# Cross attention: the value weighting moved from three places in a half to two, the last block's own buffer, and the output weights in a context buffer

## Chip, cores and metric

One core of one Trainium2 chip runs the whole program. The metric is device microseconds (us) of one execution; lower is better. The kernel before takes 4177.87 us (median of 3 runs, 4175.75 to 4178.8).

## What is computed

Four transformer layers on x (16 x 64 x 256, f32), each of cross attention, self attention and a feed-forward part. The change touches the cross attention alone, which all four layers run on the same 1601 context rows:

```python
q = split_heads(layernorm(x) @ Wq + bq)      # 16 heads of 16, 64 rows per batch
k = split_heads(ctx @ Wk + bk)               # 1601 keys
v = split_heads(ctx @ Wv + bv)
out = softmax(q k^T * scale [+ mask]) @ v    # 16 batches
x = x + merge_heads(out) @ Wo + bo
```

Layer 0 adds a float mask to the scores, layer 2 replaces masked scores, layers 1 and 3 have none.

## The kernel before

`cross_attention` works through 32 **halves** u (16 batches, two groups of 8 heads), each in seven **steps** i = 0 to 6. Every engine (PE, DVE, ACT, POOL) runs through the same list of steps in an order that is written out by hand; semaphores tie them together. The numbers of a half are kept in `prob` (128 x 4 x 1601). Before the weighting with the values, `prob` has to be transposed block by block: 1601 keys make 13 blocks of 128 rows, two to a step, the last step with a single block of 65 rows.

In step i of half u PE does, in this order:

1. `scores` (L474) of the next half, chunk i, in steps 0 to 3;
2. `turn` (L486): the transposes of two blocks of half u into PSUM banks 4 and 5. Its `bank(...)` waits until the copy of the blocks turned one step earlier is out of these banks;
3. `make_keys` (L502) of half u+2 in even steps, `make_values` (L516) of the next batch in odd ones. Both write bank 7 (UNIT), and each waits until what was there before has been taken out: for keys by `keys_low` (L671) on DVE, in layer 2 by the product with `kept` (L660), for values by `values_copy` (L609). In step 6 of odd halves a small `make_values` (the 65 rows) comes first, into bank 5;
4. `weighted` (L531): what is turned is multiplied with the values. Steps 0 to 6 are weighted in three bursts: blocks of steps 0 and 1 at the end of step 2, of steps 2 and 3 at the end of step 4, of steps 4, 5 and 6 at the end of step 0 of the next half, followed there by `spread_denominators` (L541).

The turned blocks are copied from PSUM to `prob_t` by `turned_copy` (L599): ACT takes steps 0 to 3, DVE steps 4 to 6. `prob_t` is a ring of four places, one for each step. DVE's order in step 4 is: the copy of the turned blocks (L599), then `keys_high` (L663), then `keys_low` (L671); in step 5: the copy (L599), the copy of the values (L609); in step 6 the copy of the 65 rows, in odd halves the small values, and keys again. In step 0 it takes the maxima of the scores (L641, L644), the low part of keys, and then `outputs` of the half before (L683, L686, L688), after which step 1's maxima follow. ACT computes the exponentials (L737) of the next half in steps 4 to 6. POOL splits the context into two parts (L810, L812) at steps 1, 3 and 5 of odd halves, in layer 2 the keys as well (L826, L828). In layer 2 DVE makes the next mask at the end of odd halves (L365, L368).

SP issues the loads. The output weights `wout` (256 KB) are loaded before the context of batch 1; `raw_ctx[0]` and `raw_ctx[1]` take turns for the context chunks. `project_out` (L563) reads `wout` from half 30, step 1 on.

The last half has bank 0 as a second place for the transposes (odd steps), its copies alternate between ACT and DVE.

Of the kernel before, what the change touches and what calls it, by code (L numbers as in the profile page):

```python
# [15 lines left out]
P = 128  # L16
B, S, D, H = 16, 64, 256, 16
HD = D // H
C = D // P
# [4 lines left out]
KT = -(-KEYS // P)  # L24
# [79 lines left out]
def by_rows(ap):  # L104
    return ap.rearrange("(c p) n -> p c n", p=P)
# [192 lines left out]
STEPS = (KT + 1) // 2  # L298
CH = len(KCH)
TURNED, HEADS, UNIT = 4, 6, 7  # L300
LAST = HALVES - 1
WEIGHTED_AT = {2: (0, 1), 4: (2, 3)}

def cross_attention(k, L, scale, mask=None, wo='Wo', bo='bo'):

# [2 lines left out]
    nc, ps, dram, cst = k.nc, k.ps, k.dram, k.cst  # L308
    name = f"L{L}_xattn_"
    st = Stage(k)  # L310
    wk, wv = (st.tile(n, [P, 2, C, D], F32R) for n in ('wk', 'wv'))
    raw_ctx = [st.tile(f"raw_ctx{i}", [P, C, KCH[0][1]]) for i in range(2)]
    ctx = st.tile("ctx", [P, 2, C, KEYS2], F32R)
    keys = [st.tile(f"keys{g}", [P, 2, KEYS2], F32R) for g in range(2)]
    wout = st.tile("wout", [P, C, D])
    mk = [st.tile(f"mk{i}", [P, KEYS]) for i in range(2)] if mask else None
    kept = st.tile("kept", [P, KEYS]) if mask == 'fill' else None
    vals = [st.tile(f"vals{i}", [P, KT, D]) for i in range(2)]
    prob = [st.tile(f"prob{i}", [P, ROWS, KEYS]) for i in range(2)]
    prob_t = st.tile("prob_t", [P, 4, 2, 512])  # L320
    q_heads = st.tile("q_heads", [P, C, P])
    q_parts = [st.tile(f"q_parts{i}", [P, 2, C, P], F32R) for i in range(2)]
    mx = st.tile("mx", [P, ROWS, CH])
# [14 lines left out]
    def width(i):  # L338
        return min(KCH[i][1], KEYS - KCH[i][0])

    def columns(i):
        return slice(KCH[i][0], KCH[i][0] + width(i))

    def ctx_chunk(b, i):
        return dram['ctx_t'][b].rearrange("(c p) n -> p c n", p=P)[:, :, columns(i)]

    def load_mask(b):
        sem = st[f'mask{b % 2}']
        if mask == 'add':
            nc.sync.dma_start(mk[b % 2][0:S, :], dram['mask_f'][b]).then_inc(sem, 16)  # L350
            nc.sync.dma_start(mk[b % 2][S:P, :], dram['mask_f'][b]).then_inc(sem, 16)
        else:
            nc.sync.dma_start(mk[b % 2][:].bitcast(I32), dram['mask_i'][b].partition_broadcast(P)).then_inc(sem, 16)
# [28 lines left out]
    def turn_bank(u, i):  # L382

        return 0 if u == LAST and i % 2 else TURNED

    def blocks(i):
        return [x for x in (2 * i, 2 * i + 1) if x < KT]

    def rows_of(x):
        return min(P, KEYS - x * P)  # L390

    def steps():


        for u in range(-2, HALVES):
            for i in range(STEPS):
                chunk = i // 2 if i % 2 == 0 and u + 2 < HALVES else None
                pairs = []
                if u // 2 + 1 < B:
                    pairs = [i // 2 + 3 * (u % 2)] if i % 2 else [6] if i == 6 and u % 2 else []  # L400
                yield u, i, u >= 0, 0 <= u + 1 < HALVES and i < CH, chunk, pairs
# [4 lines left out]
    def values_out(b, n):  # L406

        if values_by_act(n):
            return st.at('v_act', 4 * b + (0, 1, 3, 4).index(n) + 1)
        return st.at('v_dve', 3 * b + (2, 5, 6).index(n) + 1)  # L410

    def turned_out(u, i):

        if u == LAST:
            return st.at('pt_dve' if i % 2 else 'pt_act', (3 if i % 2 else 4) * u + i // 2 + 1)
        return st.at('pt_act', 4 * u + i + 1) if i < 4 else st.at('pt_dve', 3 * u + i - 3)
# [8 lines left out]
    def out_tiles(u, i):  # L425

        return [t for t in ([i - 1] if u == LAST - 1 else [i + 5]) if 0 <= t < T - 1 and (u < LAST or i == 1)]

    def ring(u, i):
        return (u * STEPS + i) % 4  # L430

    def sp():
        sp = nc.sync
        for n, tile, i in (('Wk', raw_wk, 0), ('Wv', raw_wv, 1), ('Wq', wq, 2)):
            sp.dma_start(tile, by_rows(dram[name + n])).then_inc(st[n], 16)
            sp.dma_start(first_ctx[:, :, columns(i)], ctx_chunk(0, i)).then_inc(st[f'first{i}'], 16)
        sp.dma_start(first_ctx[:, :, columns(3)], ctx_chunk(0, 3)).then_inc(st['first3'], 16)
        if mask:
            load_mask(0)
        sp.dma_start(wout[:], by_rows(dram[name + wo])).then_inc(st['wout'], 16)  # L440
        sp.dma_start(k.row[:], dram['bias_rows'][BIAS_ROWS.index(name + bo)].partition_broadcast(P)).then_inc(st['row'], 16)
        for b in range(1, B):
            if mask:
                if b >= 2:
                    sp.wait_ge(*st.at('nmx', 2 * (b - 1)))
                load_mask(b)
            for i in range(CH):
                if b > 1 or i >= 2:
                    sp.wait_ge(*st.at('ctx_lo', CH * b + i - 1))
                sp.dma_start(raw_ctx[i % 2][:, :, 0:width(i)], ctx_chunk(b, i)).then_inc(st[f'ctx{i % 2}'], 16)  # L450
        if L == 0:
            clear_sorted(k, st, zeros)

    def pe():
# [7 lines left out]
        def scores(h, i):  # L462
            b, g = h // 2, h % 2
            k0, kw = KCH[i]
            pe.wait_ge(*st.at('k_lo', CH * h + i + 1))
            if i == 0:
                pe.wait_ge(*st.at('q_lo', b + 1))
            for m, (qp, kp) in enumerate(PASSES):
                for r in range(ROWS):
                    if m == 0:  # L470
                        bank(r)
                        free[r] = st.at('s_out', ROWS * (CH * h + i) + r + 1)
                    rows = slice(32 * r, 32 * r + 32)
                    mm = pe.matmul(ps[:, r, 0:kw], q_parts[b % 2][rows, qp, g, :], keys[g][rows, kp, k0:k0 + kw],  # L474
                                   start=(m == 0), stop=(m == 2))
            mm.then_inc(st['s_mm'], 1)
# [43 lines left out]
        def weighted(u, i):  # L520
            b, g = u // 2, u % 2
            if i == 0:
                pe.wait_ge(*values_out(b, 4))
                pe.wait_ge(*values_out(b, 6))
                if u:
                    pe.wait_ge(*st.at('both', u))
            pe.wait_ge(*turned_out(u, i))
            for a, x in enumerate(blocks(i)):
                w = rows_of(x)
                for r in range(ROWS):  # L530
                    mm = pe.matmul(ps[32 * r:32 * r + 32, HEADS, g * P:(g + 1) * P],  # L531
                                   vals[b % 2][0:w, x, (ROWS * g + r) * 32:(ROWS * g + r + 1) * 32],
                                   prob_t[0:w, ring(u, i), a, r * P:(r + 1) * P], start=(x == 0), stop=(x == KT - 1))
            mm.then_inc(st['pv_mm'], 1)

        def spread_denominators(u):
# [31 lines left out]
        for u, i, attend, score, chunk, pairs in steps():  # L568
            if score:
                scores(u + 1, i)  # L570
            if attend:
                turn(u, i)
            if 6 in pairs:
                make_values(u // 2 + 1, 6)
            if chunk is not None:
                make_keys(u + 2, chunk)
            elif pairs:
                make_values(u // 2 + 1, pairs[0])
            if u == -2 and i in (2, 4):
                project_queries(i // 2 - 1)  # L580
            if u >= LAST - 1:
                for t in out_tiles(u, i):
                    project_out(t)
            if attend:
                for x in WEIGHTED_AT.get(i, ()):
                    weighted(u, x)
            if u >= 1 and i == 0:
                for x in (4, 5, 6):
                    weighted(u - 1, x)
                spread_denominators(u - 1)  # L590
        for x in (4, 5, 6):
            weighted(LAST, x)
        spread_denominators(LAST)
        project_out(T - 1)
# [1 line left out]
    def turned_copy(copy, sem, u, i):  # L596

        w, nb = rows_of(blocks(i)[-1]), len(blocks(i))
        copy(prob_t[0:w, ring(u, i), 0:nb, :], ps[0:w, turn_bank(u, i):turn_bank(u, i) + nb, :]).then_inc(st[sem], 1)  # L599

    def turned_ready(engine, u, i):
        n = u * STEPS + i
        engine.wait_ge(*st.at('t_mm', n + 1))
        if n >= 4:
            engine.wait_ge(*st.at('pv_mm', n - 3))

    def values_copy(copy, sem, b, n):
        w, nb = rows_of(blocks(n)[-1]), len(blocks(n))
# [181 lines left out]
    def pool():  # L790
# [48 lines left out]
        for u, i, attend, score, chunk, pairs in steps():  # L839
# [18 lines left out]
            if mask == 'add' and u >= 0 and u % 2 == 0 and i == 5 and b < B:  # L858
                mask_row(b)

    sp()
    pe()
    dve()
    act()
    pool()
    n = HALVES
# [875 lines left out]
def clear_sorted(k, st, zeros):  # L1742

    sp = k.nc.sync
    sp.wait_ge(*st.at('zeros', 1))
    for L in (2, 3):
        sp.dma_start(k.dram[f'sorted{L}'].rearrange("(s p) d -> p s d", p=P),
                     zeros[:].unsqueeze(1).broadcast_to([P, BLOCKS * 2, D])).then_inc(st[f'cleared{L}'], 16)
# [624 lines left out]
```

## Time and profile before

| What | Value |
|---|---|
| median of 3 runs | 4177.87 us (4175.75 to 4178.8) |
| the profiled execution | 4171.85 us |
| its span, first to last instruction | 4170.5 us |
| mean granted TensorE clock | 0.951 |
| PE busy | 3803.9 us (91%) |
| PEld (weight loads) busy | 3192.5 us (77%) |
| DVE busy | 2811.9 us (67%) |
| ACT busy | 2135.9 us (51%) |
| POOL busy | 1597.8 us (38%) |
| `weighted` L531, PE | 13312 records, 444.5 us |
| `turn` L486, PE | 6656 records, 916.3 us |
| copy of turned blocks L599, DVE | 384 records, 402.3 us |

PE is the matmul row and PEld the weight load row of the same engine; each f32 matmul in the program shows as two records. "Idle before" is the time an engine stood still ahead of an instruction, with what ended it; "issue" there means that it waited for no other engine.

### The profile page before, as it was taken

The numbers are of one execution on the slowest core, as the hardware profiler recorded it, in microseconds if no ns is written. First come the engines' busy times: TensorE is split into PE (matmuls) and PEld (weight loads), VectorE is DVE, ScalarE is ACT, GpSimd is POOL, SyncE is SP. The second block draws the span as 40 slices with busy tenths as digits, with TensorE's granted clock in tenths as the row PEclk, the third lists the DMA queues.
The fourth block names the chain that finished last, engine by engine and source line by source line (L and its number), as shares of the span: only waits on it lengthen the run. The fifth ranks groups of instructions, "written<-read, shape, count | busy, mean of one in ns | idle before, by whom it ended". The sixth has DMA issues, their size and how long they took to land. (4 is left out here: it accounts for less than half of the span.)

```text
span 4170.5 us, 102428 instructions
## 1 busy us (share of the span) xinstructions
PE 3803.9 (91%) x42956; PEld 3192.5 (77%) x42956; DVE 2811.9 (67%) x7243; ACT 2135.9 (51%) x2963; POOL 1597.8 (38%) x1647
## 2 busy tenths in 40 slices
PE   7999999854999999988999999986997999999866
PEld 6888888633888888857788888865996888888656
DVE  5777777676777777753777777755446777777544
ACT  4555555442555556533445454533654555555434
POOL 3444343201332332130666655513773333322146
PEclk9999999986999999998999999986998999999968
DMA  3122123001111111010211111102542111110035
GB/s 95 49 65 57 49 65 109 17 23 35 41 41 33 38 44 33 10 39 31 69 53 53 49 64 52 30 12 91 186 148 75 38 33 41 41 33 25 13 104 176
DMA packets 125594, 235.94 MB, mean 57 GB/s; under 512 B 9920, under 2 KB 114768, under 8 KB 121296
## 3 DMA queue, kind: packets, MB, share of 16 engines
q1 hardware_dynamic: 117744, 172.34, 13.9%
q0 software_dynamic: 7392, 57.06, 3.8%
q8 instruction: 341, 5.59, 0.5%
q14 instruction: 117, 0.96, 0.1%
HBM read 208.39 MB, written 20.97 MB: 55 GB/s over the span
## 5 line engine op out<-in xcount | busy, mean ns | idle before, releaser
L599 ACT COPY prob_t<-ps 128x1024 f32<-128x1024 f32 x512 | 518.4, 1013 | 1162.3 <-PE ps L486 1162.3
L486 PE MATMUL ps<-c_ident,prob 128*128 128x128 f32 (+1 forms) x6656 | 916.3, 279 | 12.7 <-ACT prob L737 9.9
L486 PEld LDWEIGHTS ps<-c_ident,prob 128*128 128x128 f32 (+1 forms) x6656 | 717.4, 141 | 188.9 <-issue 157.5
L737 ACT ACTIVATE prob<-prob,nmx 128x1601 f32<-128x1601 f32 x512 | 828.7, 1625 | 1.1 <-DVE nmx L650 1.1
L502 PE MATMUL ps<-ctx,wk 128*128 128x400 f32 (+1 forms) x3072 | 691.7, 361 | 21.9 <-DVE vals L609 14.1
L516 PE MATMUL ps<-wv,ctx 128*128 128x256 f32 x4992 | 704.4, 289 | 3.3 <-DVE vals L609 3.1
L516 PEld LDWEIGHTS ps<-wv,ctx 128*128 128x128 f32 x4992 | 619.9, 186 | 10.5 <-DVE vals L609 4.0
L641 DVE CUSTOM_DVE_ANT_0 prob<-ps,mk 128x400 f32<-128x400 f32 (+2 forms) x1024 | 526.2, 569 | 112.9 <-PE ps L474 110.4
L644 DVE TENSOR_SCALAR_CACHE_REDUCE prob<-ps 128x400 f32<-128x400 f32 (+2 forms) x1024 | 526.1, 569 | 90.9 <-PE ps L474 90.7
L502 PEld LDWEIGHTS ps<-ctx,wk 128*128 128x128 f32 x3072 | 534.8, 191 | 45.3 <-DVE vals L609 28.5
L599 DVE COPY prob_t<-ps 128x1024 f32<-128x1024 f32 (+1 forms) x384 | 402.3, 1048 | 239.1 <-PE ps L486 238.8
L810 POOL CAST ctx<-raw_ctx 128x804 fp32r<-128x804 f32 x240 | 205.2, 855 | 735.8 <-PE ps L502 735.8
L474 PE MATMUL ps<-keys,q_parts 32*128 32x400 f32 (+1 forms) x6144 | 474.3, 379 | 5.3
L531 PE MATMUL ps<-prob_t,vals 128*32 128x128 f32 x13312 | 444.5, 275 | 1.2 <-DVE prob_t L599 1.2
L531 PEld LDWEIGHTS ps<-prob_t,vals 128*32 128x32 f32 x13312 | 339.8, 110 | 102.2 <-issue 99.4
L812 POOL TENSOR_TENSOR ctx<-raw_ctx,ctx 128x804 fp32r<-128x804 f32 x240 | 402.8, 1678 | 19.3
L852 POOL TENSOR_TENSOR diag<-c_ident,rden 128x128 f32<-128x128 f32 x512 | 188.8, 400 | 502.5 <-DVE rden L678 502.5
L474 PEld LDWEIGHTS ps<-keys,q_parts 32*128 32x128 f32 x6144 | 274.4, 183 | 137.7 <-issue 70.3
L671 DVE SCALAR_TENSOR_TENSOR keys<-ps,cols,keys 128x400 fp32r<-128x400 f32 (+2 forms) x384 | 243.4, 634 | 129.0 <-ACT keys L743 121.8
L2108 POOL TENSOR_TENSOR parts<-raw,parts 128x1368 fp32r<-128x1368 f32 (+2 forms) x70 | 205.1, 2938 | 68.3 <-ACT parts L2033 67.7
L609 ACT COPY vals<-ps 128x512 f32<-128x512 f32 x256 | 149.5, 584 | 128.7 <-PE ps L516 128.7
L1982 PE MATMUL ps<-x_parts,parts 128*114 128x256 f32 (+1 forms) x1440 | 189.0, 289 | 14.3 <-POOL parts L2108 7.3
(350 smaller groups left out, 4313.0 us busy)
## 6 DMA issues: line engine op xcount, KB each, us to landing
raw_ctx<-in_ctx_t SPq DMA_DIRECT2D x120, 400.0 KB, 3.3
raw_ctx<-in_ctx_t SPq DMA_DIRECT2D x60, 402.0 KB, 5.1
raw_ctx<-in_ctx_t SPq DMA_DIRECT2D x60, 399.0 KB, 3.3
mk<-in_mask_f SPq DMA_DIRECT2D x32, 400.2 KB, 5.5
mk<-in_mask_i SPq DMA_DIRECT2D x16, 800.5 KB, 4.4
sorted<-zeros SPq DMA_DIRECT2D x2, 3840.0 KB, 20.6
rows<-sorted SPq DMA_DIRECT2D x30, 256.0 KB, 5.2
done<-done SPq DMA_DIRECT2D x30, 256.0 KB, 2.5
```

What stands on the lines that cost most here:

```text
L474: mm = pe.matmul(ps[:, r, 0:kw], q_parts[b % 2][rows, qp, g, :], keys[g][rows, kp, k0:k0 + kw], start=(m == 0), stop=(m == 2))
L486: mm = pe.transpose(ps[0:w, turn_bank(u, i) + a, r * P:(r + 1) * P], prob[u % 2][:, r, x * P:x * P + w], cst['ident'][:])
L502: mm = pe.matmul(ps[:, to, 0:kw], wk[:, wp, c, g * P:(g + 1) * P], ctx[:, xp, c, k0:k0 + kw], start=(c == 0 and m == 0), stop=(c == C - 1 ...
L516: mm = pe.matmul(ps[0:w, to, a * D:(a + 1) * D], ctx[:, xp, c, x * P:x * P + w], wv[:, wp, c, :], start=(c == 0 and m == 0), stop=(c == C ...
L531: mm = pe.matmul(ps[32 * r:32 * r + 32, HEADS, g * P:(g + 1) * P], vals[b % 2][0:w, x, (ROWS * g + r) * 32:(ROWS * g + r + 1) * 32], prob_ ...
L599: copy(prob_t[0:w, ring(u, i), 0:nb, :], ps[0:w, turn_bank(u, i):turn_bank(u, i) + nb, :]).then_inc(st[sem], 1)
L641: v.tensor_tensor_reduce(o, ps[:, r, 0:vw], mk[b % 2][:, k0:k0 + vw], 1.0, NEG, ALU.add, ALU.max, mx[:, r, i:i + 1]).then_inc(st['s_out'], 1)
L644: v.tensor_scalar(o, ps[:, r, 0:vw], 0.0, NEG, ALU.add, ALU.max, accum_out=mx[:, r, i:i + 1]).then_inc(st['s_out'], 1)
L671: v.scalar_tensor_tensor(keys[g][:, 1, k0:k0 + vw], ps[:, key_bank(h, i), 0:vw], k.col(name + 'bk')[:, g:g + 1], keys[g][:, 0, k0:k0 + vw] ...
L737: a.activation(prob[h % 2][:, r, :], prob[h % 2][:, r, :], ACT.Exp, bias=nmx[:, r:r + 1], accum_out=den[h % 2][:, r:r + 1]).then_inc(st['e ...
L810: p.tensor_copy(ctx[:, 0, :, columns(i)], raw).then_inc(st['ctx_own'], 1)
L812: p.tensor_tensor(ctx[:, 1, :, columns(i)], raw, ctx[:, 0, :, columns(i)].bitcast(F32), ALU.subtract).then_inc(st['ctx_lo'], 1)
```

## The change

`weighted` runs in two bursts in place of three: blocks of steps 0, 1 and 2 at the end of step 2, blocks of steps 3 to 6 at the end of step 0 of the next half. The ring of four places holds steps 0 to 5, and step 6's single block gets a tile of its own, `last_t`. The conditions on which a copy may write are counted anew. `wout` loses its tile and is loaded into `raw_ctx[0]`, behind all context chunks. The code:

```diff
-WEIGHTED_AT = {2: (0, 1), 4: (2, 3)}
+WEIGHTED_AT = {2: (0, 1, 2)}
+CARRIED = (3, 4, 5, 6)
+RING = 4
...
-    wout = st.tile("wout", [P, C, D])
+    wout = raw_ctx[0][:, :, 0:D]
...
-    prob_t = st.tile("prob_t", [P, 4, 2, 512])
+    prob_t, last_t = st.tile("prob_t", [P, RING, 2, 512]), st.tile("last_t", [P, 1, 512])
...
-    def ring(u, i):
-        return (u * STEPS + i) % 4
+    def turned(u, i):
+
+        return last_t if i == STEPS - 1 else prob_t[:, (u * (STEPS - 1) + i) % RING]
...
-        sp.dma_start(wout[:], by_rows(dram[name + wo])).then_inc(st['wout'], 16)
...
+        sp.wait_ge(*st.at('ctx_lo', CH * B - 1))
+        sp.dma_start(wout, by_rows(dram[name + wo])).then_inc(st['wout'], 16)
...
             if u >= 1 and i == 0:
-                for x in (4, 5, 6):
+                for x in CARRIED:
                     weighted(u - 1, x)
                 spread_denominators(u - 1)
-        for x in (4, 5, 6):
+        for x in CARRIED:
             weighted(LAST, x)
...
     def turned_ready(engine, u, i):
-        n = u * STEPS + i
-        engine.wait_ge(*st.at('t_mm', n + 1))
-        if n >= 4:
-            engine.wait_ge(*st.at('pv_mm', n - 3))
+        n = u * (STEPS - 1) + i
+        engine.wait_ge(*st.at('t_mm', u * STEPS + i + 1))
+        if i == STEPS - 1:
+            if u:
+                engine.wait_ge(*st.at('pv_mm', u * STEPS))
+        elif n >= RING:
+            old_u, old_i = divmod(n - RING, STEPS - 1)
+            engine.wait_ge(*st.at('pv_mm', old_u * STEPS + old_i + 1))
```

On PE, before, from step 3 of half 1 of layer 0 to the end of its step 6 (prob_14 is what is turned, vals_11 the batch's values; each matmul counts once here):

```order
L474 MATMUL ps<-keys_6,q_parts_18 128x400 x12
L486 MATMUL ps<-c_ident,prob_14 128x128 x8
L516 MATMUL ps<-wv,ctx 128x256 x12
L486 MATMUL ps<-c_ident,prob_14 128x128 x8
L502 MATMUL ps<-ctx,wk 128x400 x6
L531 MATMUL ps<-prob_t,vals_11 32x128 x16
L486 MATMUL ps<-c_ident,prob_14 128x128 x8
L516 MATMUL ps<-wv,ctx 128x256 x12
L486 MATMUL ps<-c_ident,prob_14 65x128 x4
L516 MATMUL ps<-wv,ctx 65x256 x6
L502 MATMUL ps<-ctx,wk 128x400 x6
```

The same place in the changed kernel (lines are four higher, prob_14 is now prob_13):

```order
L478 MATMUL ps<-keys_6,q_parts_18 128x400 x12
L490 MATMUL ps<-c_ident,prob_13 128x128 x8
L520 MATMUL ps<-wv,ctx 128x256 x12
L490 MATMUL ps<-c_ident,prob_13 128x128 x8
L506 MATMUL ps<-ctx,wk 128x400 x6
L490 MATMUL ps<-c_ident,prob_13 128x128 x8
L520 MATMUL ps<-wv,ctx 128x256 x12
L490 MATMUL ps<-c_ident,prob_13 65x128 x4
L520 MATMUL ps<-wv,ctx 65x256 x6
L506 MATMUL ps<-ctx,wk 128x400 x6
```

The burst of 16 between the keys of step 4 and the transposes of step 5 is gone.

On PE, in the changed kernel, the end of step 0 of the next half and what follows (before, the burst read `L531 MATMUL ps<-prob_t,vals_11 32x128 x20`):

```order
L506 MATMUL ps<-ctx,wk 128x402 x6
L535 MATMUL ps<-prob_t,vals_10 32x128 x24
L535 MATMUL ps<-last_t,vals_10 32x128 x4
L545 MATMUL ps<-diag,c_pairblk 32x128 x4
L478 MATMUL ps<-keys_7,q_parts_18 128x400 x12
```

This burst has grown by 8 matmuls; the burst at the end of step 2 has grown by 8 too, from 16 to 24.

## Rows read from the trace of the kernel before

**Rows 1.** The page's first part: busy us (share of the span) xrecords.

```profile
PE 3803.9 (91%) x42956; PEld 3192.5 (77%) x42956; DVE 2811.9 (67%) x7243; ACT 2135.9 (51%) x2963; POOL 1597.8 (38%) x1647
```

**Rows 2.** Line L531 (PEld): what ended its idle time, us, times.

```profile
  issue: 99.4, 384
```

**Rows 3.** Timeline, layer 0, odd half, steps 4 to 6 (start, us, engine, line).

```profile
322.02 0.90 PEld L486 LDWEIGHTS ps<-c_ident,prob 128*128 128x128 f32 x8
...
322.96 1.02 PEld L502 LDWEIGHTS ps<-ctx,wk 128*128 128x128 f32 x6
...
323.20 1.23 DVE L599 COPY prob_t<-ps 128x1024 f32<-128x1024 f32 x1 [0.94 <-PE ps L486]
324.25 0.81 PEld L531 LDWEIGHTS ps<-prob_t,vals 128*32 128x32 f32 x32 [0.26 <-issue]
...
324.36 0.63 DVE L663 TENSOR_SCALAR keys<-ps,cols 128x400 fp32r<-128x400 f32 x1
...
325.02 0.63 DVE L671 SCALAR_TENSOR_TENSOR keys<-ps,cols,keys 128x400 fp32r<-128x400 f32 x1
325.26 0.86 PEld L486 LDWEIGHTS ps<-c_ident,prob 128*128 128x128 f32 x8 [0.20 <-issue]
...
326.08 1.49 PEld L516 LDWEIGHTS ps<-wv,ctx 128*128 128x128 f32 x12
...
326.39 1.22 DVE L599 COPY prob_t<-ps 128x1024 f32<-128x1024 f32 x1 [0.73 <-PE ps L486]
...
327.67 0.41 PEld L486 LDWEIGHTS ps<-c_ident,prob 128*65 128x65 f32 x4
...
328.74 1.04 PEld L502 LDWEIGHTS ps<-ctx,wk 128*128 128x128 f32 x6
```

**Rows 4.** Timeline, layer 0, even half: steps 5 and 6, into the next half.

```profile
303.37 1.47 PEld L516 LDWEIGHTS ps<-wv,ctx 128*128 128x128 f32 x12
...
305.83 1.03 PEld L502 LDWEIGHTS ps<-ctx,wk 128*128 128x128 f32 x6 [0.46 <-DVE vals L609]
...
306.48 0.19 ACT L737 ACTIVATION_READ_ACCUMULATOR prob<-prob,nmx 128x1 f32 x1
...
307.88 0.86 PEld L486 LDWEIGHTS ps<-c_ident,prob 128*128 128x128 f32 x8 [0.26 <-issue]
```

**Rows 5.** Timeline, layer 0, steps 0 and 1 of an odd half.

```profile
311.14 1.90 POOL L812 TENSOR_TENSOR ctx<-raw_ctx,ctx 128x804 fp32r<-128x804 f32 x1
...
312.31 0.82 DVE L688 SCALAR_TENSOR_TENSOR XNT<-both,cols 128x64 f32<-128x64 f32 x1
...
314.63 0.21 PEld L474 LDWEIGHTS ps<-keys,q_parts 32*128 32x128 f32 x3
...
315.16 0.47 PEld L474 LDWEIGHTS ps<-keys,q_parts 32*128 32x128 f32 x9 [0.31 <-DVE mx L641]
...
315.89 0.85 PEld L486 LDWEIGHTS ps<-c_ident,prob 128*128 128x128 f32 x8 [0.26 <-issue]
```

**Rows 6.** The same of an even half: `outputs`, scores of step 2, next transposes.

```profile
718.57 0.28 DVE L688 SCALAR_TENSOR_TENSOR XNT<-both,cols 128x64 f32<-128x64 f32 x1
...
720.90 0.49 PEld L474 LDWEIGHTS ps<-keys,q_parts 32*128 32x128 f32 x12
...
721.65 0.85 PEld L486 LDWEIGHTS ps<-c_ident,prob 128*128 128x128 f32 x8 [0.26 <-issue]
```

**Rows 7.** Timeline, layer 0, half 30 (no keys or values left), steps 5 and 6.

```profile
751.71 0.86 PEld L486 LDWEIGHTS ps<-c_ident,prob 128*128 128x128 f32 x8 [0.20 <-issue]
...
754.12 0.41 PEld L486 LDWEIGHTS ps<-c_ident,prob 128*65 128x65 f32 x4 [0.85 <-DVE prob_t L599]
```

**Rows 8.** Timeline, layer 2: end of an odd half, and scores of an even half's step 2.

```profile
2107.33 1.60 POOL L812 TENSOR_TENSOR ctx<-raw_ctx,ctx 128x800 fp32r<-128x800 f32 x1
...
2109.18 0.98 DVE L365 TENSOR_SCALAR mk<-mk 128x1601 f32<-128x1601 int32 x1
...
2092.22 2.21 PE L474 MATMUL ps<-keys,q_parts 32*128 32x400 f32 x12
```

More of the change, by code:

```diff
@@ L532, in weighted @@
                                    vals[b % 2][0:w, x, (ROWS * g + r) * 32:(ROWS * g + r + 1) * 32],
-                                   prob_t[0:w, ring(u, i), a, r * P:(r + 1) * P], start=(x == 0), stop=(x == KT - 1))
+                                   turned(u, i)[0:w, a, r * P:(r + 1) * P], start=(x == 0), stop=(x == KT - 1))
             mm.then_inc(st['pv_mm'], 1)
@@ L598, in turned_copy @@
         w, nb = rows_of(blocks(i)[-1]), len(blocks(i))
-        copy(prob_t[0:w, ring(u, i), 0:nb, :], ps[0:w, turn_bank(u, i):turn_bank(u, i) + nb, :]).then_inc(st[sem], 1)
+        copy(turned(u, i)[0:w, 0:nb, :], ps[0:w, turn_bank(u, i):turn_bank(u, i) + nb, :]).then_inc(st[sem], 1)
     def turned_ready(engine, u, i):
-        n = u * STEPS + i
-        engine.wait_ge(*st.at('t_mm', n + 1))
-        if n >= 4:
-            engine.wait_ge(*st.at('pv_mm', n - 3))
+        n = u * (STEPS - 1) + i
[6 more added lines that the diff above has]
+            engine.wait_ge(*st.at('pv_mm', old_u * STEPS + old_i + 1))
     def values_copy(copy, sem, b, n):
```

## The prediction, written before the changed kernel was run

> **What bounds the kernel now.** I read the page's first part first. PE is busy for 91% of the span, no other engine for more than 67% [rows 1]. So the first question is what PE's order costs. The busy share itself cannot say what a moved burst is worth; for that I read the timeline of one half, engine by engine, and ask at each instruction what let it start. The halves are regular: the times of one, told from the start T of the transposes of step 4 (322.02 in [rows 3]), recur in the others within a few hundredths.
>
> In [rows 3] the reader is to see two things. First, the weighting burst stands between two gaps in which PE waits for nobody: 0.26 us before it and 0.20 after it. The source view counts such gaps before a burst: 99.4 us in 384, three for each of 128 halves [rows 2]. Second, while the burst runs, DVE works off a chain of three: the copy of the turned blocks (ends T+2.41), `keys_high`, and `keys_low`, which ends at 325.65 = T+3.63. The transposes of step 5 need the first of these, the values of step 5 the third, since they write the bank that the keys were in. Both start later than that today (T+3.24 and T+4.06), so neither waits. The burst is their cover.
>
> **What is removed.** In each half the burst of step 4 goes, with one pair of gaps: 0.26 + 0.20 = 0.46 us. Its 0.81 us of loads do not go. Half of them, 0.41, are added at the end of step 2, the other half at the end of step 0, where a burst with its gaps stands anyway. If PE had nothing to wait for, keys to transposes would cost a gap of up to 0.1, and a half would gain about 0.37.
>
> **What takes its place, layers 0, 1 and 3.** I follow PE from T. The keys of step 4 are loaded by T+1.96. The transposes of step 5 would come now, but banks 4 and 5 are free only when DVE's copy is done, T+2.41. From the end of such a copy to PE's next start takes 0.06 (326.39 + 1.22 = 327.61, then 327.67 [rows 3]), so they start at T+2.47. That copies cannot be beaten is seen in half 30, where nothing stands between: the next transposes start 2.41 after the ones before, and DVE's copy is named as what they waited for [rows 7]. Next, PE reaches the values 0.82 later, as today (325.26 to 326.08), at T+3.29, and waits for `keys_low`: T+3.63 + 0.06 = T+3.69. Today they start at T+4.06, of which 0.82 is moved work, so T+3.24 would be even. **The loss at this point is 0.45 us**: all of the gaps' 0.46 is given back, and as much again.
>
> In even halves nothing mends it: the keys of step 6 start 2.46 after the values of step 5 and are already released by DVE's copy of the values [rows 4], so the whole 0.45 goes through. In odd halves the transposes of step 6 wait today for the copy (327.67). Changed, that copy starts T+3.60 and is out by T+4.82, while PE gets there at about T+5.2; before it was T+5.65, less 0.82. So 0.39 is left of the 0.45. The small values and the keys behind them run on PE's own time. The exponentials do not enter: they end 306.67, and the transposes that need them start 307.88, 1.21 later [rows 4]; 0.4 of that is used up. Each layer has 15 even and 15 odd halves with keys and values to make (0 to 29): 15 x 0.45 + 15 x 0.39 = 12.6 us, three layers 37.8.
>
> **What is swallowed.** The 0.41 added in step 0 lies ahead of `outputs` on DVE, and of the scores of step 2 on PE. In odd halves PE stalls there today: from the scores' first load to the next transposes takes 1.26 us [rows 5], in even halves 0.75 [rows 6]. The cause is L688: 0.82 us in the odd half, 0.28 in the even; it ends at 313.13, just after POOL's L812 at 313.04. L812 follows the keys of step 0, not the burst. So the burst may grow by 0.41: L688 starts at 312.72, still ends at 313.13, and the scores are released when they were. By the Trainium skill, page "SBUF — State Buffer", section "Who interferes with whom", a DVE instruction with two SBUF inputs and a GpSimd instruction that reads SBUF exclude each other for a whole instruction; the trace agrees with the 0.82 against 0.28. POOL has that work in 14 odd halves a layer (1 to 27): 3 x 14 x 0.41 = 17.2 us come off. The 0.41 in step 2 finds no stall and counts in full; it is already in the 0.82.
>
> **Layer 2.** DVE has one instruction between copy and values there (L660) where the others have two, so values wait for PE alone, and a half loses 0.05: 30 x 0.05 = 1.5. The stall of the scores in step 2 is in the even halves (2.21 us of matmuls [rows 8]), since the mask is made on DVE just before: 14 x 0.41 = 5.7 off. But at the end of odd halves everything comes 0.77 earlier from T (0.82 less 0.05), while POOL's L812 stays (ends 2108.93) and the mask's L365 (2109.18 [rows 8]) would start at 2108.41. If the two exclude each other as L688 and L812 do, it loses up to 0.5 in 14 halves: 6.6. No row shows this pair; from nothing to 6.6, I take 6.6, as the nearest case, L688 behind L812, shows a full wait [rows 5]. Layer 2: +1.5 - 5.7 + 6.6 = +2.4.
>
> **Halves 30 and 31.** No keys or values are left, PE waits for ACT and DVE, and the burst of step 4 was hidden. Three pieces of 0.41 come ahead of the chain and the third block of step 2 waits for its copy; a later transpose takes part of it back. Bounds 0 and 1.6 a layer; I take 1.0, so 4.1 for four.
>
> **At nothing**: the later load of the output weights (256 KB) is issued in half 27 and first read in half 30; its cover are the halves between, and PE would stand still for a landing only if that cover were gone. The ring of four now holds six steps of a half, and every copy's place is weighted at least one step earlier than needed. DVE's order is unchanged.
>
> **Sum**: 37.8 - 17.2 + 2.4 + 4.1 = +27.1 us. The profiled execution took 4171.85 us (span 4170.5), 6 below the median; the sum moves it to 4199.0, and the median from 4177.87 to **4205.0 us**.
>
> **The rivals.**
> *The gaps win, 0.09.* If DVE's chain did not hold PE back, 120 halves would gain 0.37 (44 us), the swallowed 17.2 and 5.7 stay, the tail costs 4.1: 63 less, 4115. It decides from the point where `keys_low` ends before T+3.2. The Trainium skill, "TensorEngine Tiling (Array Packing)", "Key Properties", says that a change of tiling mode drains TensorE, and fewer changes are what this edit buys; the gaps of 0.26 and 0.20 agree with it. Against: both waits are in the program, and DVE's ends do not depend on the burst.
> *Only the first wait bites, 0.12.* If the values behaved in all layers as in layer 2, a half would lose 0.05: 3 x (1.5 - 5.7) + 2.4 + 4.1 = -6, so 4172. For it: DVE's instructions start up to 0.07 before the one ahead ends (324.36 against 324.43 [rows 3]), so the chain may be shorter where PE presses on it. Against: `keys_low` ends at T+3.63 whatever PE does.
> *Nothing is swallowed, 0.08.* If step 0's 0.41 delays all that follows, through L688 or the maxima behind it, 23 come back: +50, 4228. Against: L688's end follows POOL, not the burst.
>
> **How the numbers follow.** The forecast has 0.71. Its own range: swallowing and layer 2's mask by their ends, 4186 to 4226. To hold 8 in 10 the range reaches a little toward the second rival: 4181 to 4228. A measurement can tell about 0.2%, 8.4 us, from no change. Slower is the forecast and the third rival, 0.79; no change the second rival with the forecast's low edge, 0.12; faster the first, 0.09.
>
> **What would show it.** In the changed profile, L531's gaps ahead of bursts should number 256. The transposes of step 5 should carry an idle time ended by DVE `prob_t` L599, and the values of step 5 one of 0.3 to 0.5 ended by DVE `keys` (L671 before), the latter not in layer 2. From T to the values should be 3.69, to the keys of step 6 6.16 in even halves. L688 should take 0.4 in odd halves, not 0.82, and the scores' stall there be gone. If no idle time stands before these values, the forecast is wrong; if the stall at the scores has moved by 0.41 instead of vanishing, the sum is too small.

## The result, and the profile after

The changed kernel takes 4205.74 us (median of 6 runs, 4198.86 to 4209.32), the kernel before 4175.84 us in the same comparison: a ratio of 1.0071, 95% interval 1.0058 to 1.0084, 29.9 us slower. The forecast was 4205.0 us and +27.1. The profiled execution took 4198.86 us, its span is 4197.5 us against 4170.5, at a granted clock of 0.952 against 0.951. So the clock is not the cause. Line numbers shift by a few from one kernel to the next; tile names tell which instruction is meant.

The page of the changed kernel, first its parts of the engines, then the costliest groups (out<-in xcount | busy, mean ns | idle time of the engine before them and what ended most of it):

```profile
PE 3792.8 (90%) x42956; PEld 3196.6 (76%) x42956; DVE 2794.2 (67%) x7243; ACT 2134.6 (51%) x2963; POOL 1596.6 (38%) x1647
...
L490 PEld LDWEIGHTS ps<-c_ident,prob 128*128 128x128 f32 (+1 forms) x6656 | 723.6, 141 | 220.7 <-issue 132.0
...
L520 PEld LDWEIGHTS ps<-wv,ctx 128*128 128x128 f32 x4992 | 618.2, 185 | 46.1 <-DVE keys L679 37.0
```

The work is the same ([rows 1] against the first line); what has grown is time in which PE stands still: of the 27.0 us between the two spans, 22.9 are idle time of the weight-load row (span less busy time), 4.1 longer loads. The grouped view by line has the releasers in full. Before, the same two groups read:

```profile
L486 PEld LDWEIGHTS ps<-c_ident,prob 128*128 128x128 f32 (+1 forms) x6656 | 717.4, 141 | 188.9 <-issue 157.5 <-ACT prob L737 12.9 <-DVE prob_t L599 3.4
L516 PEld LDWEIGHTS ps<-wv,ctx 128*128 128x128 f32 x4992 | 619.9, 186 | 10.5 <-DVE vals L609 4.0 <-issue 3.3 <-DVE keys L671 1.6
```

and in the changed kernel:

```profile
L490 PEld LDWEIGHTS ps<-c_ident,prob 128*128 128x128 f32 (+1 forms) x6656 | 723.6, 141 | 220.7 <-issue 132.0 <-DVE prob_t L603 67.5 <-ACT prob L745 14.9
L520 PEld LDWEIGHTS ps<-wv,ctx 128*128 128x128 f32 x4992 | 618.2, 185 | 46.1 <-DVE keys L679 37.0 <-DVE vals L617 4.0 <-issue 3.3
```

The transposes (L486, now L490) wait 67.5 us for DVE's copy where they waited 3.4, and the values (L516, now L520) 37.0 us for `keys_low` where they waited 1.6. Against this stand the gaps that went: ahead of the bursts there are now 256, not 384 ([rows 2]), and they sum to 65.7 us, not 99.4; ahead of the transposes 25.5 us of such gaps went too ("issue" 157.5, now 132.0):

```profile
  issue: 65.7, 256
```

The timeline of the place that the argument was made at, an odd half of layer 0 (T = 324.18), against [rows 3]:

```profile
324.18 0.90 PEld L490 LDWEIGHTS ps<-c_ident,prob 128*128 128x128 f32 x8
...
325.12 1.02 PEld L506 LDWEIGHTS ps<-ctx,wk 128*128 128x128 f32 x6
...
325.36 1.23 DVE L603 COPY prob_t<-ps 128x1024 f32<-128x1024 f32 x1 [0.96 <-PE ps L490]
326.52 0.64 DVE L671 TENSOR_SCALAR keys<-ps,cols 128x400 fp32r<-128x400 f32 x1
...
326.64 0.85 PEld L490 LDWEIGHTS ps<-c_ident,prob 128*128 128x128 f32 x8 [0.49 <-DVE prob_t L603]
...
327.19 0.63 DVE L679 SCALAR_TENSOR_TENSOR keys<-ps,cols,keys 128x400 fp32r<-128x400 f32 x1
...
327.88 1.49 PEld L520 LDWEIGHTS ps<-wv,ctx 128*128 128x128 f32 x12 [0.39 <-DVE keys L679]
```

The step-5 transposes start at T+2.46 and name DVE's copy; the values start at T+3.70 and name `keys_low`, which ended at T+3.64. Steps 0 and 1 of an odd half, against [rows 5]:

```profile
312.85 1.91 POOL L820 TENSOR_TENSOR ctx<-raw_ctx,ctx 128x804 fp32r<-128x804 f32 x1
...
314.45 0.39 DVE L696 SCALAR_TENSOR_TENSOR XNT<-both,cols 128x64 f32<-128x64 f32 x1
...
316.77 0.57 PEld L478 LDWEIGHTS ps<-keys,q_parts 32*128 32x128 f32 x12
...
317.60 0.86 PEld L490 LDWEIGHTS ps<-c_ident,prob 128*128 128x128 f32 x8 [0.26 <-issue]
```

`outputs` now comes late enough: L696 (L688 before) is held for 0.1 us, not 0.54, and from the scores of step 2 to the next transposes it is 0.83 us, not 1.26.

### The profile page after: what moved, and what is told of

It is laid out like the page before. It is cut to its first block and busy times, and to the rows that moved or that the text cites. A ratio compares the mean times of both kernels' runs of the same rounds, so it can differ in the third digit from the quotient of the medians.

```text
span 4197.5 us, 102424 instructions
## 1 busy us (share of the span) xinstructions
PE 3792.8 (90%) x42956; PEld 3196.6 (76%) x42956; DVE 2794.2 (67%) x7243; ACT 2134.6 (51%) x2963; POOL 1596.6 (38%) x1647
## 5 line engine op out<-in xcount | busy, mean ns | idle before, releaser
L490 PE MATMUL ps<-c_ident,prob 128*128 128x128 f32 (+1 forms) x6656 | 911.9, 279 | 36.4 <-DVE prob_t L603 18.2
L490 PEld LDWEIGHTS ps<-c_ident,prob 128*128 128x128 f32 (+1 forms) x6656 | 723.6, 141 | 220.7 <-issue 132.0
L520 PE MATMUL ps<-wv,ctx 128*128 128x256 f32 x4992 | 705.3, 289 | 17.4 <-DVE keys L679 9.9
L520 PEld LDWEIGHTS ps<-wv,ctx 128*128 128x128 f32 x4992 | 618.2, 185 | 46.1 <-DVE keys L679 37.0
L478 PE MATMUL ps<-keys,q_parts 32*128 32x400 f32 (+1 forms) x6144 | 460.1, 377 | 3.1
L603 DVE COPY prob_t<-ps 128x1024 f32<-128x1024 f32 x260 | 318.3, 1224 | 147.7 <-PE ps L490 147.4
L535 PE MATMUL ps<-prob_t,vals 128*32 128x128 f32 x12288 | 389.6, 275 | 0.4
L535 PEld LDWEIGHTS ps<-prob_t,vals 128*32 128x32 f32 x12288 | 319.3, 110 | 67.7 <-issue 65.7
## 6 DMA issues: line engine op xcount, KB each, us to landing
sorted<-zeros SPq DMA_DIRECT2D x2, 3840.0 KB, 19.5
```

The lines of the kernel that those rows point to most:

```text
L490: mm = pe.transpose(ps[0:w, turn_bank(u, i) + a, r * P:(r + 1) * P], prob[u % 2][:, r, x * P:x * P + w], cst['ident'][:])
L520: mm = pe.matmul(ps[0:w, to, a * D:(a + 1) * D], ctx[:, xp, c, x * P:x * P + w], wv[:, wp, c, :], start=(c == 0 and m == 0), stop=(c == C ...
L603: copy(turned(u, i)[0:w, 0:nb, :], ps[0:w, turn_bank(u, i):turn_bank(u, i) + nb, :]).then_inc(st[sem], 1)
```

## The experiments

All times are medians; each ratio is to the kernel before, run on the same chip beside it, with its 95% interval. Diffs are against the changed kernel unless said.

### The buffers and the late load alone

```diff
-WEIGHTED_AT = {2: (0, 1, 2)}
-CARRIED = (3, 4, 5, 6)
+WEIGHTED_AT = {2: (0, 1), 4: (2, 3)}
+CARRIED = (4, 5, 6)
```

> Changed kernel with the old order of the bursts (steps 2, 4 and 0), keeping the last block's own buffer, the new ring and the late load of the output weights. Theory (all of the loss comes from the lost cover on PE): the time of the kernel before, 4176 us, within 8. Rival (the late load or the new ring's conditions cost time): 4190 to 4206.

Measured: 4173.73 us, ratio 0.9997 (0.9988 to 1.0005). The new ring, the last block's own place and the output weights in a context buffer cost nothing that can be measured (the interval reaches from 5 us less to 2 us more). So the 30 us come from the order.

### Each pair of blocks moved by itself

Only step 3's pair leaves step 4, for step 0:

```diff
-WEIGHTED_AT = {2: (0, 1, 2)}
+WEIGHTED_AT = {2: (0, 1), 4: (2,)}
```

> Only the block pair of step 3 leaves step 4 for step 0; step 4 keeps a burst of one pair with both gaps. Theory: cover for DVE's chain is just enough (values of step 5 at T+3.69 where 3.65 would be even, 0.03 to 0.04 lost in 90 halves, 3 us), and the 0.41 us added in step 0 is swallowed where POOL holds L696 (17 us) and in layer 2's even halves (6 us), less 4 us for the tail and layer 2's mask: 4160 us. Rival (nothing is swallowed, the added work delays all that follows): 4180 us or more.

Only step 2's pair leaves step 4, for step 2:

```diff
-WEIGHTED_AT = {2: (0, 1, 2)}
-CARRIED = (3, 4, 5, 6)
+WEIGHTED_AT = {2: (0, 1, 2), 4: (3,)}
+CARRIED = (4, 5, 6)
```

> Only the block pair of step 2 leaves step 4, for the end of step 2, where no stall can swallow it. Theory: 3 us for the chain, 2 for layer 2's mask, 4 for the tail: 4185 us. Rival (swallowing has nothing to do with the place): the same time as the kernel in which only the pair of step 3 moves.

Measured: 4160.34 us, ratio 0.9960 (0.9944 to 0.9976), and 4187.15 us, ratio 1.0028 (1.0017 to 1.0038). Half a burst, taken from the same place, makes the kernel 0.4% faster where step 0 takes it and 0.3% slower where step 2 does. Both keep a burst of one pair in step 4, so no gap is saved in either. In the first, the step-5 transposes start without a wait:

```profile
320.06 1.02 PEld L506 LDWEIGHTS ps<-ctx,wk 128*128 128x128 f32 x6
321.34 0.38 PEld L535 LDWEIGHTS ps<-prob_t,vals 128*32 128x32 f32 x16 [0.26 <-issue]
321.92 0.86 PEld L490 LDWEIGHTS ps<-c_ident,prob 128*128 128x128 f32 x8 [0.20 <-issue]
322.81 1.47 PEld L520 LDWEIGHTS ps<-wv,ctx 128*128 128x128 f32 x12
```

Nothing is named there but the gaps of 0.26 and 0.20: half the burst is all the cover that DVE's chain needs, to within 0.1 us a half. The two changes sum to -13.4 + 13.4 = 0 us against the kernel before; both together are +30. So about 30 us is the price of taking the last of the cover away, and this is already net of the pair of gaps that goes with it.

The medians of whole executions hide something here. From the first transposes of half 0 to the last of half 31, summed over the four layers, the traces have 2843.8 us for the kernel before, 2843.3 for the buffers alone, 2824.9 and 2852.0 for the two pairs moved singly, and 2874.7 for the changed kernel: -18.9, +8.2 and +30.9. By this sum the last cover costs 42 us, not 30. The rest of the program, which no edit touches, took between 1320 and 1335 us in the traced executions. So a difference of a few us between two of these kernels can't be put down to an edit by the whole time alone.

### Where POOL makes the stall

Against the kernel before, in layers 0, 1 and 3:

```diff
             p.wait_ge(*st.at(f'ctx{i % 2}', 16 * (2 * (b - 1) + i // 2 + 1)))
+            if mask != 'fill' and i == 0 and b >= 2:
+                p.wait_ge(*st.at('heads', 2 * b - 3))
```

> Kernel before; in layers 0, 1 and 3 POOL's first context part of an odd half waits until outputs (L688) of the half before is done. Theory (L688 and L812 exclude each other, and this makes the stall of 0.51 us at the scores of step 2): L688 takes 0.28 in odd halves, the stall is gone, 42 x 0.51 = 21 us less: 4153 us. Rival (the stall has another cause, or POOL's later end delays keys): 4174 us or more.

Measured: 4151.53 us, ratio 0.9940 (0.9926 to 0.9954). One added wait makes the kernel before 0.6% faster. Its odd half:

```profile
308.81 0.28 DVE L688 SCALAR_TENSOR_TENSOR XNT<-both,cols 128x64 f32<-128x64 f32 x1
...
309.23 0.86 POOL L812 CAST ctx<-raw_ctx 128x804 fp32r<-128x804 f32 x1 [7.37 <-DVE XNT L688]
...
311.14 0.49 PEld L474 LDWEIGHTS ps<-keys,q_parts 32*128 32x128 f32 x12
311.89 0.85 PEld L486 LDWEIGHTS ps<-c_ident,prob 128*128 128x128 f32 x8 [0.26 <-issue]
```

L688 takes 0.28 us, and from the scores to the next transposes it is 0.75. (POOL's lines are two higher here: this L812 is the cast that was L810.) All 32 instances of L688 in layer 0 take 0.28 us now; before, 14 of them took 0.82. So the stall comes from L688 running beside POOL's context part. The Trainium skill, "SBUF — State Buffer", section "Who interferes with whom", says that a DVE instruction with two SBUF inputs contends with a GpSimd instruction that reads SBUF, and calls the port pair that they share an exclusive lock. The trace agrees: L688 reads two parts of `both`, and takes 0.82 beside POOL and 0.28 apart from it. That this is the stall which swallows the pair moved to step 0 is tested below.

### The two waits taken away

The values of step 5 go to score bank 3, which no one uses in steps 4 to 6:

```diff
         if n == 6:
             return TURNED + 1
+        if b and n in (2, 5):
+            return 3
```

> Changed kernel, but the values of step 5 are written to score bank 3, which is free in steps 4 to 6, so they no longer wait for keys_low, nor the keys of step 6 for the copy of the values. Theory: values start at T+3.29, where PE is ready; even halves end 0.28 ahead of before (then the exponentials hold the next transposes), odd ones 0.05 behind; with the swallowed 0.41: about 4150 us. Rival (the wait on keys_low is not what costs; PE is held by the copy or something else anyway): 4195 to 4206 us.

Measured: 4153.16 us, ratio 0.9948 (0.9935 to 0.9961): 52.6 us less than the changed kernel, from a bank number. Not all of this is the lost cover. The bank also frees the keys of step 6 from their wait for the copy of the values, and that wait stands in the kernel before as well. The keys' group in the kernel before, in the changed one and in this one:

```profile
L502 PEld LDWEIGHTS ps<-ctx,wk 128*128 128x128 f32 x3072 | 534.8, 191 | 45.3 <-DVE vals L609 28.5 <-issue 5.3 <-ACT XNT L165 3.2
L506 PEld LDWEIGHTS ps<-ctx,wk 128*128 128x128 f32 x3072 | 535.1, 191 | 51.3 <-DVE vals L617 33.5 <-issue 6.0 <-ACT XNT L165 3.2
L508 PEld LDWEIGHTS ps<-ctx,wk 128*128 128x128 f32 x3072 | 535.2, 191 | 17.9 <-issue 6.2 <-ACT XNT L165 3.2 <-DVE keys L681 2.9
```

The step-5 transposes still wait for the copy, the values no longer for anything:

```profile
320.79 0.85 PEld L492 LDWEIGHTS ps<-c_ident,prob 128*128 128x128 f32 x8 [0.48 <-DVE prob_t L605]
321.61 1.48 PEld L522 LDWEIGHTS ps<-wv,ctx 128*128 128x128 f32 x12
```

Besides, the transposes of step 5 into banks 0 and 1:

```diff
-        return 0 if u == LAST and i % 2 else TURNED
+        return 0 if i == 5 or (u == LAST and i % 2) else TURNED
```

> Changed kernel, values of step 5 in bank 3 and the transposes of step 5 in banks 0 and 1, so that PE waits neither for keys_low nor for DVE's copy of step 4. Theory: now the removed gaps of 0.46 us pay. Even halves are capped at 0.28 by the exponentials, odd ones gain about 0.43; with the swallowed 0.41: about 4121 us. Rival (another engine's chain, DVE's copies themselves, sets the half's length, so the banks bring little more): 4145 to 4153 us.

Measured: 4127.22 us, ratio 0.9889 (0.9873 to 0.9905). This is 6 us above the 4121 expected. PE now waits 84.4 us of weight-load idle time for the exponentials (12.9 in the kernel before).

The same two bank changes under the old order of the kernel before, and with only step 3's pair moved:

> Kernel before with the same two bank changes and its old order of bursts. Theory: the cover hides both waits already; only the small waits for the copy of the values (even halves, 0.5 us) and at the transposes of step 6 (0.06) go: about 4139 us. Against the run with the changed order this prices the order alone, once its waits are gone: about 18 us. Rival (the banks are worth the same with either order): 4121 us, or no gain at all, 4174 us.

> Only the pair of step 3 moved to step 0, with the two bank changes. Theory: 4139 less the swallowed 17 and 6, plus 4 for tail and mask: about 4120 us, the same as the changed order with these banks, since there the exponentials cap even halves. Rival (the gaps, not the swallowed work, are what matters): 4135 us or more, well behind the run with two bursts.

Measured: 4129.93 us, ratio 0.9893 (0.9879 to 0.9908), and 4110.65 us, ratio 0.9839 (0.9826 to 0.9853). Two misses by 9 us, both on the fast side: with bank 4 left alone in step 5, the transposes of step 6 start 2.23 us behind those of step 5 where it was 2.41, and I had allowed 0.06 for it.

The first of these and the run before it price the order: they differ in nothing else but the new buffers, and those cost nothing. With the old banks it costs 29.9 us, with the two waits gone it gains 2.7 (4129.93 less 4127.22, the intervals overlap): so the waits account for some 33 us, and without them the order is not slower. They also show that more than half of the 79 us that the banks bring the changed order has nothing to do with it: under the old order they bring 44.

Why 2.7 and not the expected 18? By the traces the same stretch of halves gets 15.1 us shorter in layers 0, 1 and 3 together, near the forecast, and 9.9 us longer in layer 2 (713.6 to 723.5). In layers 0, 1 and 3 the even halves lose to the exponentials: the wait for them is 12.9 us in all under the old order and 84.4 under the new.

```profile
L488 PEld LDWEIGHTS ps<-c_ident,prob 128*128 128x128 f32 (+1 forms) x6656 | 724.9, 141 | 173.5 <-issue 157.2 <-ACT prob L739 12.9 <-ACT prob_t L601 2.6
```

In layer 2 it is step 0 of the even halves that grows, from 4.87 to 5.78 us where the added work explains 0.44; what holds it there was not tested. Moving only step 3's pair does better than the whole change, by 16.6 us: I had expected the two to be even.

### The exponentials

Two of the next three build on the changed order with both bank changes. First, the keys of step 4 in score bank 2, and ACT copies step 3's values behind the first exponential:

```diff
-        return (UNIT, TURNED + 1, TURNED, UNIT)[i] if h < 2 else UNIT
+        return (UNIT, TURNED + 1, TURNED, UNIT)[i] if h < 2 else 2 if i == 2 else UNIT
...
                 for r in ((0, 1), (2,), (3,))[i - 4]:
                     exponentials(u + 1, r)
+                    if r == 0 and b < B:
+                        copy_late(b, 1 + 3 * (u % 2))
```

> The run with the changed order and both bank changes, and besides the keys of step 4 in score bank 2 and ACT's copy of step 3's values behind the first exponential. Theory: the exponentials, which hold PE for 45 us in all in the run without this, start 0.55 us earlier in about 60 halves: 4127 less 33, about 4094 us, ahead of the run in which only the pair of step 3 moves (4111). Rival (the late copy of the values or DVE holds PE next): 4115 to 4127 us.

Measured: 4107.73 us, ratio 0.9841 (0.9828 to 0.9855). My expectation failed by 14 us, and the grouped view says how: the weight loads of the transposes still wait 78.8 us for ACT, against 84.4. The copy only changed places with an exponential, and the last of the four, for which PE waits, seems to end when ACT's sum of work is done; the last run below bears this out. What did come, 19.5 us between the medians, lies with 12.6 us in the halves, by the sum used above (the keys of step 4 no longer wait for ACT's copy, and from the transposes of step 4 to those of step 5 it is 1.89 us where it was 1.97); the rest was not located.

The next adds POOL's wait to this version. The one behind it adds POOL's wait to the version with both banks and only step 3's pair moved.

> The same with POOL's wait for outputs. Theory: the stall at the scores of step 2 is swallowed already but for 0.1 us in 42 halves: 4 us less than without, if nothing else. Rival (swallowing and removing the stall add up): 20 us less.

> Pair of step 3 moved, both bank changes, and POOL's wait for outputs. Theory: as before, the stall is swallowed but for 0.1 us: 4111 less 4, about 4107 us. Rival (they add up): 4090 us.

Measured: 4106.96 us, ratio 0.9847 (0.9833 to 0.9860), and 4107.47 us, ratio 0.9840 (0.9826 to 0.9854), each within its run-to-run spread of the same kernel without the wait. What is worth 22 us in the kernel before is worth 0.8 and 3.2 here, so swallowing and removing the stall do not add up: they are the same 0.5 us.

Last, on the changed order with both banks and the keys of step 4 in bank 2 (without the late copy), DVE copies step 3's values, at the head of its step 4, and ACT's part of this copy is gone (the wait of `weighted` for ACT's last values and the counts follow):

```diff
-        return n in (0, 1, 3, 4)
+        return n in (0, 3)
...
+            if i == 4 and b < B:
+                n = 1 + 3 * (u % 2)
+                v.wait_ge(*st.at('v_mm', 7 * b + n + 1))
+                values_copy(v.tensor_copy, 'v_dve', b, n)
             if i == 4 and attend:
                 denominators(u)
```

> Changed order of bursts, both bank changes, the keys of step 4 in score bank 2, and the copy of step 3's values given from ACT to DVE, which stands still for 0.95 us there. Theory (after the copy only moved behind the first exponential had left ACT's sum of work and so the last exponential where they were): now the last one ends 0.55 us earlier, and the exponentials no longer hold the transposes: about 20 to 35 us less than the 4127 of the run with ACT's copy ahead, 4092 to 4107 us, even or ahead of the run with only step 3's pair moved (4111). Rival (DVE becomes the next bound, its copy of step 4 starts later): 4115 us or more.

Measured: 4078.55 us, ratio 0.9766 (0.9753 to 0.9779). This is the fastest version, 96 us ahead of the kernel before. The same group, with both bank changes alone, then with the late copy, then with DVE's:

```profile
L492 PEld LDWEIGHTS ps<-c_ident,prob 128*128 128x128 f32 (+1 forms) x6656 | 735.0, 141 | 195.5 <-issue 99.6 <-ACT prob L747 84.4 <-DVE prob_t L605 2.7
```

```profile
L492 PEld LDWEIGHTS ps<-c_ident,prob 128*128 128x128 f32 (+1 forms) x6656 | 733.6, 140 | 190.0 <-issue 99.7 <-ACT prob L747 78.8 <-DVE prob_t L605 2.7
```

```profile
L492 PEld LDWEIGHTS ps<-c_ident,prob 128*128 128x128 f32 (+1 forms) x6656 | 733.5, 140 | 159.2 <-issue 115.6 <-ACT prob L751 32.0 <-DVE prob_t L605 2.7
```

Against the first of these it is 48.7 us of time, where I had expected 20 to 35. But 19.5 of that had come with the run before, whose keys of step 4 this one keeps, and I had not counted it. Giving the copy to DVE is worth the other 29.2 us, inside the range. The rows agree: from the second line to the third the waits for ACT fall by 46.8 us, gaps that they had covered come back ("issue", 15.9 more), and the group's idle time falls by 30.8. The matmul row of the same two runs falls by 30.9 in its wait for ACT:

```profile
L492 PE MATMUL ps<-c_ident,prob 128*128 128x128 f32 (+1 forms) x6656 | 900.8, 277 | 42.6 <-ACT prob L747 39.9 <-DVE prob_t L605 1.8 <-ACT prob_t L605 0.9
L492 PE MATMUL ps<-c_ident,prob 128*128 128x128 f32 (+1 forms) x6656 | 900.4, 277 | 12.1 <-ACT prob L751 9.0 <-DVE prob_t L605 1.8 <-ACT prob_t L605 0.9
```

So it is the idle time of the whole group that tells the time, not one releaser's share of it. No run has this last step under the old order or with only step 3's pair moved, so how much of the 96 us the order contributes stays open.

## Why the prediction was right

- **The gaps are given back, as much again is lost.** Forecast: transposes of step 5 at T+2.47, values at T+3.69. In 15 even and 15 odd halves of each of layers 0, 1 and 3 the medians are T+2.45 and T+3.70. The profile names the copy and `keys_low`. In layer 2, where no second DVE instruction stands between, the values start at T+3.28 and the loss is 0.05, as forecast. That these two waits make the order slow is shown by the pair of runs with both banks: without the waits the same change of order costs nothing.
- **Even 0.45, odd 0.39.** The keys of step 6 start at T+6.17 in even halves (forecast 6.16), and at T+6.24 in odd ones: losses of 0.47 and 0.33. I had taken PE's arrival at the transposes of step 6 for T+5.2; it is 5.1.
- **Swallowed 17.2 us.** From the transposes of step 0 to those of step 2 an odd half takes 8.01 before and 8.02 after, though the burst between has grown; an even one 7.52 and 7.95. So it was swallowed, and the runs with POOL's wait, worth 22 us where the work has not moved and 1 to 3 where it has, show it to be this stall. The burst grew by 0.43 to 0.44, not 0.41: the mean of a record within a burst had not told what eight instructions more would take.
- **Layer 2: +2.4 forecast, +4.9 measured** over 29 halves. The pair without a row was real: the mask on DVE runs beside POOL's context part now and takes 1.39 us against 0.98 in [rows 8], 0.41 lost where I had taken 0.47:

```profile
2127.60 1.61 POOL L820 TENSOR_TENSOR ctx<-raw_ctx,ctx 128x800 fp32r<-128x800 f32 x1
...
2128.67 1.39 DVE L367 TENSOR_SCALAR mk<-mk 128x1601 f32<-128x1601 int32 x1
```

  What I missed is the other side of the swallowing. In layer 2's odd halves `outputs` came just ahead of POOL's context part:

```profile
2043.35 0.28 DVE L688 SCALAR_TENSOR_TENSOR XNT<-both,cols 128x64 f32<-128x64 f32 x1
...
2043.44 0.91 POOL L810 CAST ctx<-raw_ctx 128x804 fp32r<-128x804 f32 x1
```

  0.44 later it comes behind it, is held to POOL's end (2063.71), and a stall of some 0.25 us stands where none was. L696 takes 0.58 in 13 of these halves, so this is some 3 us in all:

```profile
2062.86 0.85 POOL L818 CAST ctx<-raw_ctx 128x804 fp32r<-128x804 f32 x1
...
2063.20 0.58 DVE L696 SCALAR_TENSOR_TENSOR XNT<-both,cols 128x64 f32<-128x64 f32 x1
```

- **Layers 0, 1 and 3**: 37.8 - 17.2 = 20.6 us forecast; +7.4, +6.8 and +6.5, together 20.6, measured from the first to the last full half, 654.14 to 661.51 us in layer 0. Here the larger bursts (+0.03 in each) and the smaller loss in odd halves cancel: that the sums agree to 0.1 us is luck, the terms are off by 1 to 3 us each.
- **The last halves**: 4.1 forecast; +1.0, +1.0, +0.7 and +1.0, together 3.7.
- **At nothing**: the load and the buffers, confirmed by the first experiment.
- The rivals: *the gaps win* needs the two waits gone, which only other banks do; *only the first wait bites* is refuted by the values' start at T+3.70 and their 37.0 us of waits for `keys_low`; *nothing is swallowed* by the 8.01 and 8.02 us of the odd halves and by the runs with POOL's wait.

By terms, 20.6 + 4.9 + 3.7 = 29.2 us against 29.9 measured between the medians, and 27.0 between the two spans; the rest of the program differs by 2 us between two single executions.

## What to carry to other kernels

Before a piece of work is taken out of its place on the bound engine, look at what the other engines do while it runs: if a chain there ends when the piece ends, it is cover, and removing it turns its time into waits. Look for the resource that makes the wait (here a PSUM bank) and change that first, where another phase leaves one free: two bank numbers made the old order 1.1% faster than before, and the new one, 0.7% slower until then, 1.1% faster too; with the next chain shortened it was 2.3%. Price the order with and without its waits before you keep it. Where added work lands matters as much as where it leaves: half a burst was worth -13 us in one step and +13 in another.

## What the runs showed of the hardware

That POOL and DVE hold each other up cost more than the instructions suggest: a 64-column sum on DVE, 0.28 us by itself, was held 0.54 us behind POOL, and in this chain PE passed it on almost in full, 22 us of 4174. Adding a wait to the engine with time to spare removed it. I had not expected the exclusion to turn over within 0.44 us: in layer 2, DVE's instruction starts 0.09 us ahead of POOL's before the change (2043.35 and 2043.44) and takes 0.28; afterwards POOL's starts first (2062.86 and 2063.20), and DVE's takes 0.58.
